# Two attention stages: the row of maxima issued from ScalarE's queue, and no extra products on TensorE

## The reference, cut to what matters

```python
x = layernorm(x + attn0(x))     # 16 heads of width 8, rotary, causal mask, then Wproj
x = layernorm(x + moe_ffn(x))   # 7 experts, top 2, and a shared one
x = layernorm(x + attn1(x))     # 16 heads of width 8, rotary, no mask, no projection
x = layernorm(x + dense_ffn(x))
# in both attentions, for each batch and head:
scores = q @ k.T / sqrt(8)
y = softmax(scores) @ v
```

## Time and profile before

| | |
|---|---|
| time, three runs | 1503.41, 1495.87, 1502.93 us; median 1502.93 |
| profiled execution | 1501.69 us, its span 1500.0 us |
| granted TensorE clock, mean | 0.891 of 2.4 GHz |
| busy: TensorE, VectorE, ScalarE, GpSimd | 83%, 61%, 53%, 35% |
| DMA: packets, moved | 55948, 53.26 MB |

### The profile page before, as it was taken

One profiled execution on the slowest core, in us unless ns is written; L12 is line 12 of the kernel. 1 busy time (PEld: TensorE's weight loads), 2 busy tenths in 40 slices (PEclk: granted clock), 3 DMA queues, 4 the chain that ended last, 5 costly groups with the idle time before them and its releaser, 6 DMA issues. The chain is left out here.

```text
span 1500.0 us, 28689 instructions
## 1 busy us (share of the span) xinstructions
PE 1239.8 (83%) x10443; PEld 726.8 (48%) x10443; DVE 921.8 (61%) x2838; ACT 788.9 (53%) x1543; POOL 521.6 (35%) x476
## 2 busy tenths in 40 slices
PE   3588977877798597794399899899898969999996
PEld 1344434434454464672144344343343447888885
DVE  3556855866673766445388788788787642334542
ACT  1144644644554663443137676676676745556553
POOL 3324523532511455573513033033030004445553
PEclk9988977988878598897559899999999989999998
DMA  4212113202300401333340310310321000000000
GB/s 101 29 39 45 28 18 44 34 13 44 44 2 2 130 15 41 109 62 66 42 108 15 44 34 12 44 36 11 44 31 15 2 15 8 15 14 14 14 21 15
DMA packets 55948, 53.26 MB, mean 36 GB/s; under 512 B 8000, under 2 KB 38720, under 8 KB 55824
## 3 DMA queue, kind: packets, MB, share of 16 engines
q1 hardware_dynamic: 51808, 48.33, 16.2%
q0 software_dynamic: 3696, 2.76, 1.3%
q10 hardware_dynamic: 320, 0.52, 0.1%
HBM read 15.74 MB, written 8.06 MB: 16 GB/s over the span
## 5 line engine op out<-in xcount | busy, mean ns | idle before, releaser
L433 ACT ACTIVATE a_prob<-a_ps_s 128x512 f32<-128x512 f32 (+1 forms) x896 | 466.4, 565 | 340.3 <-PE a_ps_s L514 336.1
L600 DVE TENSOR_REDUCE a_mx<-a_ps_m 128x1 f32<-128x512 f32 x512 | 327.9, 682 | 87.7 <-PE a_ps_m L529 86.3
L529 PE MATMUL a_ps_m<-a_kst,a_qst 24*128 24x512 f32 (+3 forms) x1024 | 284.1, 480 | 43.8 <-DMA a_qst<-a_lo_q 36.8
L597 DVE CUSTOM_DVE_ANT_0 a_junk<-a_ps_m,maskw 128x384 f32<-128x384 f32 (+3 forms) x512 | 227.2, 486 | 148.6 <-PE a_ps_m L529 148.5
L514 PE MATMUL a_ps_s<-a_qst,a_kst 25*128 25x512 f32 (+3 forms) x1024 | 246.4, 464 | 76.9 <-DMA a_qst<-a_mrow 67.4
L551 PE MATMUL a_ps_o<-a_prob,a_vst 128*32 128x256 f32 (+2 forms) x3840 | 286.6, 387 | 2.9 <-ACT a_oT L441 2.1
L514 PEld LDWEIGHTS a_ps_s<-a_qst,a_kst 25*128 25x128 f32 x1024 | 110.9, 193 | 230.8 <-ACT a_prob L433 95.7
L371 POOL TENSOR_SCALAR_AFFINE_SELECT a_prob<-a_prob 128x512 f32<-128x512 f32 x128 | 80.1, 638 | 265.6 <-ACT a_prob L433 265.6
L465 PE MATMUL a_ps_s<-a_kst 128*32 128x256 f32 x2000 | 169.8, 414 | 0.0
L529 PEld LDWEIGHTS a_ps_m<-a_kst,a_qst 24*128 24x128 f32 x1024 | 129.1, 200 | 72.1 <-issue 40.4
L551 PEld LDWEIGHTS a_ps_o<-a_prob,a_vst 128*32 128x32 f32 x3840 | 86.8, 113 | 106.4 <-issue 71.2
(11 more groups left out here) (292 smaller groups left out, 1933.2 us busy)
## 6 DMA issues: line engine op xcount, KB each, us to landing
a_kst<-a_hi_k SPq DMA_DIRECT2D x128, 64.0 KB
a_qst<-a_hi_q SPq DMA_DIRECT2D x128, 64.0 KB
f_w<-in_L_ffn_W_dram SPq DMA_DIRECT2D x21, 256.0 KB, 3.6
a_kst<-a_lo_k SPq DMA_DIRECT2D x64, 64.0 KB
a_qst<-a_lo_q SPq DMA_DIRECT2D x64, 64.0 KB
x_tiles<-in_L_attn_x_dram SPq DMA_DIRECT2D x8, 256.0 KB, 4.6
normed_rows_dram<-f_nrm SPq DMA_DIRECT2D x8, 256.0 KB, 2.3
f_hT_hi<-expert_sums_dram SPq DMA_DIRECT2D x4, 512.0 KB, 6.0
```

The source lines that it names most:

```text
L433: act.activation(prob[k][:, i, 0:w], ps_s[g % SB][:, 0:w], ACT.Exp, scale=float(D) ** -0.5)\
L529: last = pe.matmul(ps_m[g % MB][:, col:col + w], qst[r][lo_row:end, t, P * j:P * j + P], kst[r][lo_row:end, t, 0:w], start=True, stop=True)
L597: ins = dve.tensor_tensor_reduce(junk[g % MB][:, col:col + w], bank[:, col:col + w], maskw[:, T - w:T], 1.0, -3.0e38, ALU.add, ALU.max, out)
L600: ins = dve.reduce_max(out, bank[:, col:col + w], AX.X)
```

## The change

SyncE loses `max_row` altogether. Its order is now one stack after the other, and in stage two `ahead` stands right behind the first stack. ScalarE issues the same DMA, with the same tiles and semaphores, directly behind the copy that makes `mrow`, after waiting for that copy. On TensorE `warm` and its calls are gone. Nothing else moves, and what is computed is the same.

```diff
-                def max_row(n):
-
-                    b, t = divmod(n, NG)
-                    sp.wait_ge(s_read["maxT"], n + 1)
-                    sp.dma_start(qst[b % 2][KROWS:P:QUAD, t, :].bitcast(F32).rearrange("i (j q) -> i j q", j=QT),
-                                 mrow[n % 2][:, :].bitcast(F32)).then_inc(s_mst, 16)
-
                 stack(0)
-                max_row(0)
                 if ahead is not None:
                     ahead(sp)
-                for n in range(G):
-                    if n + 1 < G:
-                        max_row(n + 1)
-                    if n % NG == 0 and n // NG + 1 < B:
-                        stack(n // NG + 1)
+                for b in range(1, B):
+                    stack(b)
...
                     ins.then_inc(s_read[name], 1)
+                    if name == "maxT":
+                        b, t = divmod(n, NG)
+                        act.wait_ge(s_read["maxT"], n + 1)
+                        act.dma_start(qst[b % 2][KROWS:P:QUAD, t, :].bitcast(F32).rearrange("i (j q) -> i j q", j=QT),
+                                      mrow[n % 2][:, :].bitcast(F32)).then_inc(s_mst, 16)
...
-                def warm(n, u):
-
-                    g = n * U + u + 1
-                    r, t = min(n + 1, G - 1) // NG % 2, min(n + 1, G - 1) % NG
-                    after(pe, s_exp, g - SB + 1)
-                    for i in range(HG):
-                        pe.matmul(ps_s[g % SB][VW * i:VW * i + VW, 0:2 * P], kst[r][:, t, VW * i:VW * i + VW].bitcast(F32),
-                                  kst[r][:, t, 0:2 * P].bitcast(F32), start=True, stop=True)
...
                                 values(n - back, j, half)
-                                if half == 1 and (n, u) != (G - 1, U - 1):
-                                    warm(n, u)
```

## The result

| | before | after |
|---|---|---|
| median of the runs | 1500.82 (1495.87 to 1503.41, four) | 1538.59 (1533.31 to 1540.01, four) |
| ratio | | 1.0249, 95% interval 1.021 to 1.0289 |
| profiled execution, its span | 1501.69, 1500.0 | 1537.34, 1535.6 |
| granted TensorE clock, mean | 0.891 | 0.780 |

The forecast was 1414, the range 1380 to 1470. The time is outside it, on the other side, 8.6 us above the third rival's 1530.

The account below looks back on a forecast made before the run. The prediction took the stack of K and Q to bound each batch. Gains of 39 and 33 us in inner batches, 8 and 1 in first, 7 in last made 88: 1501.7 - 88 = 1414 us, range 1380 to 1470.

Parts of the forecast that it names:

- third rival: Stage two: without extra products the clock stays at 1.2 GHz, +54 us; stage one keeps perhaps 25: 1530 us; chance 0.07.
- What bounds the kernel: Each batch waits for its stacked K and Q: lag to the start, some 25.5 us of transfer, then two groups.
- the stack's term: SyncE without the rows starts each inner batch's stack earlier: 5.4 us gained in stage one, 4.4 in stage two.
- S: The moment when the previous batch's scores are all done and the next stack may overwrite the old one.
- ScalarE's issue: Issuing the row costs ScalarE 0.5 to 0.9 us a group; counted as 0.3 in two groups per stage two batch.
- The products: Deleting 250 sets of extra products gains, net of clock, 1.1 us per inner batch in stage one, 1.7 in stage two.
- The sum: Gains of both edits added over inner, first and last batches of both stages: 88 us.
- The row among the stack's packets: The row gets no lane of its own and needs none, with over 9 us between its copy and first use.

Follow-up runs that it names:

- stack_held: `rows_moved` with one more wait on SyncE, so each stack starts no earlier than in the kernel before; 1509.4 us, ratio 1.007.
- rows_moved: The changed kernel with the extra products (`warm` and its call) put back, so only the rows' move to ScalarE remains; 1450.2 us, ratio 0.967.
- rows_gpsimd: `rows_moved` with the rows of maxima issued from GpSimd's queue instead of ScalarE's, extra products kept; 1432.1 us, ratio 0.954.
- gpsimd_pause: `rows_gpsimd` with one more ScalarE copy per group, read by nobody, behind the copy of the maxima; 1435.0 us, ratio 0.957.
- rows_gpsimd_bare: The changed kernel (no extra products) with the rows issued from GpSimd's queue instead of ScalarE's; 1495.8 us, ratio 0.996.
- gpsimd_held_half: `rows_gpsimd` with the second stack's Q part held until row 0 is copied, and extra products of 128 columns instead of 256; 1428.4 us, ratio 0.942.
- mixed_sets: `rows_gpsimd` with the second stack's Q part held until row 0 is copied, extra products 256 columns in stage one, 128 in stage two; 1432.7 us, ratio 0.946.

## Why the prediction was wrong, point by point

Each stretch by its first and last scores in the two profiled runs (before minus after, so a gain is positive):

| stretch | forecast | measured |
|---|---|---|
| stage one, first batch (with its start) | +8 | 50.6 - 41.4 - 8.3 = +0.9 |
| stage one, six inner batches | +39 | 6 x (53.49 - 51.43) = +12.4 |
| stage one, last | +3 | 39.8 - 47.3 = -7.5 |
| stage two, first | +1 | 52.1 - 59.0 = -6.9 |
| stage two, six inner | +33 | 6 x (56.26 - 59.21) = -17.7 |
| stage two, last | +4 | 46.9 - 61.1 = -14.2 |
| between and behind the stages | 0 | -2.6 |
| sum | +88 | -35.6 |

*What bounds the kernel, and the stack's term: right.* The stack starts within 0.7 us of S in every batch, the waits for the row went, and `stack_held` brings back the time. The stack's share was put at 5.4 and 4.4 a batch. In `rows_moved` an inner batch of stage one takes 46.5 us on average instead of 53.5, 7.0 less, since the avoided wait had also cost clock (16 us of a batch at half clock before, 6 in `rows_moved`); in stage two `rows_gpsimd`, without ScalarE's price, has 52.3 instead of 56.3, 4.0 less.

*ScalarE's issue: mechanism right, size wrong.* The step "I take 0.3 us for each of the two uncovered groups of a batch" came to 0.6 a batch of stage two. Group by group, `rows_gpsimd` has medians of 13.0, 11.9, 14.8 and 12.7 us there and `rows_moved` 13.6, 12.1, 15.2 and 13.2: it is paid in all four, and the batches' means differ by 2.05 (54.32 - 52.27). 18 us in the whole where 4 were counted. "ScalarE has 3 us of slack in 12.6" is a mean over a group. The pause delays what ScalarE has queued behind it at that moment, and TensorE, which has three score banks to run ahead in, waits: in stage two of `rows_moved` 9.4 us for the copy of `a_oT` and 3.8 for exponentials, beside 0.5 and none in `rows_gpsimd`. The Trainium skill, "DMA: Bandwidth & Descriptors", section "Issuing engines are not separate DMA queues", says that the time an issue takes on a sequencer is usually small beside the DMA. Here it wasn't small for the engine that issues: 0.54 us, and 0.71 with the wait, of a ScalarE on which TensorE depends.

*The products: the step that failed.* It counted their deletion as a gain of 1.1 and 1.7 us a batch, net of the clock. Between `rows_moved` and the changed kernel they are a loss of 5.0 (51.43 - 46.48) and 4.9 (59.21 - 54.32). The text had the right rows: 19.86 of 20 us busy at 0.50 without the sets, and "every return inside the groups happened with the extra products running". From that it concluded 6 more microseconds at half clock in the third group. Measured in the changed kernel, the low clock of stage two went from 52 to 247 us, in groups of all four kinds: a third group of stage two's inner batches has a median of 17.5 us, of which 13.8 on average are low. Two errors lie in that. Its bounds let at most 2 and 0.5 us a batch be lost, because they priced only the third group and took the clock of the others as safe since they had it before, with the products running. And it priced the return as late, where without the products it mostly doesn't come before the third group ends. By the rule of the Trainium skill that the prediction quoted ("TensorE: Matmul & The Clock Gate", section "What's actually happening") the products were paid for; the runs agree, by 24 to 88 us. What in the products' work holds the clock, no run here shows: TensorE was busy nearly without a gap at 0.50 too.

*The two parts together.* The sum added them. They share one resource, TensorE's uninterrupted work: the pause opens gaps, and without the products the gaps cost clock. 18 us become 43. That is 25 of the 64 us of interaction. The other 40 appear already between SyncE's queue and GpSimd's, where the missing products cost 24 and 64 us: beside the stack's wait, part of their price was hidden. The runs do not separate how.

*The row among the stack's packets.* That it needs no lane of its own held but for the first row of each stage and 0.4 us in one group. In stage one the sum had promised 8 us there: the wait of 5.12 at 91.75 did go, and one of 7.11 came at 73.90, because the second stack now stands ahead of row 0. The order's piece on SyncE in the part on the change shows it for a later stack; the very first group wasn't followed to its landing.

*The rivals.* The third had the right mechanism and sign at 0.07. Its size was near by luck: a whole stage two at half clock (+54) against a kept 25 in stage one. Measured were +39 in stage two, of which 247 us of 475 ran low, and 6 kept at the end of stage one. Its group at half clock, 15.8 us, was fair: the last batch, low throughout, has 15.5, 16.0, 15.5 and 14.1. The point from which it was to decide, 360 us more at half clock, was too far off: 342 more (262 + 247 - 115 - 52) ate 124 us (88 + 36), some of it ScalarE's price, so 88 are eaten at some 250.

## What to carry to other kernels

Work that nobody reads can hold a clock: before deleting it, look for a stretch of the same trace that runs without it (here 20 us before the first scores) and price every group at the clock of that stretch, also those that have no wait now. A DMA issue moved to another engine's queue costs that engine its own wait and its issue, in every period, unless the slack is at that very place; move it to an engine that nobody waits for (here GpSimd). And two edits that both open or close gaps on the clocked engine have to be run apart and together, since their prices don't add.

## What the runs showed of the hardware

- Without the products TensorE ran at 0.50 for stretches as long as 23.9 us (905.49 to 929.38) while busy 23.77 of them, with products that use 24 or 25 rows or 32 columns of the array. It was granted 1.00 for whole batches of the same work where the extra products ran between.
- An 8 KB row issued from GpSimd's queue (`rows_gpsimd`) landed 1.7 us after its issue with no stack in flight, up to 8.8 us with one, and 10.7 us when it was issued just behind the last of a stack's 24 transfers, although these were on SyncE's queue. On ScalarE's queue the trace has no landings; of the changed kernel's rows the last packet ended 1.3 us after the issue with no stack in flight and up to 8.1 us with one, and in the case just named 9.5. The issue of the same row took 0.54 us on ScalarE and 0.58 on GpSimd.
- Consecutive activations overlap: behind a copy of 0.61 us the next exponential started 0.52 us after the copy had (`gpsimd_pause`), and with a wait for the end of the small copy ahead of it the whole pause grew from 0.68 to 0.88 us.
- Some of these kernels vary more from run to run than others: 29 us over ten runs of `rows_gpsimd_bare`, 30 over four of `gpsimd_held_half` and 33 over six of `mixed_sets`, against 17 over thirteen runs of the kernel before and 7 over four of the changed one. It does not go by the products being there or not; the reason is open.
